# Expert phase of a transformer block on one core: rows routed in normalised form, first layer in two-part weights, 39 tiles in place of 40

## What is computed

```python
x = x + layernorm(attention(layernorm(x)))
x = x + layernorm(ffn(layernorm(x)))

def ffn(f):                                   # f = layernorm(x), 128 wide
    expert = argmax(f @ centroids.T)
    alpha  = sigmoid(max score)
    h = (f - mean(f)) * rsqrt(var(f) + 1e-5) * gamma[e] + beta[e]
    y = f + relu(h @ W1[e].T + b1[e]) @ W2[e].T + b2[e]     # hidden width 512
    return alpha * y + (1 - alpha) * f
```

## Time and profile before

| | us |
|---|---|
| median of 3 timed runs | 1307.07 (1305.11 to 1332.18) |
| the profiled execution: its time | 1304.03 |
| its span, first to last instruction | 1302.2 |
| attention phase, to the last matrix product of a block | to about 1083 |
| handover (last block's routing, filling rows, table) | about 1083 to 1104 |
| expert phase, first load to last store | 1103.9 to 1293.9 |

### The profile page before, as it was taken

One profiled execution on the slowest core, in us unless ns is written; L12 is line 12 of the kernel. 1 busy time (PEld: TensorE's weight loads), 2 busy tenths in 40 slices (PEclk: granted clock), 3 DMA queues, 4 the chain that ended last, 5 costly groups with the idle time before them and its releaser, 6 DMA issues.

```text
span 1302.2 us, 40447 instructions
## 1 busy us (share of the span) xinstructions
PE 1239.2 (95%) x12156; PEld 1101.3 (85%) x12156; DVE 1157.4 (89%) x4556; ACT 1058.5 (81%) x3176; POOL 923.2 (71%) x1442
## 2 busy tenths in 40 slices
PE   6999999999999999999999999999999995999992
PEld 4898999989998998889899899989999884788782
DVE  4999999999999999999999999999999883799993
ACT  4998888888888888888888888888888882666661
POOL 3567777777777777777777777777777563488886
PEclk8999999999999999999999999999999996999996
DMA  5000000000000000000000000000000003121120
GB/s 221 6 10 14 13 12 12 12 12 12 12 12 12 12 12 12 12 12 12 12 12 12 12 12 12 12 12 12 12 8 9 10 10 84 50 64 59 58 61 4
DMA packets 38504, 31.88 MB, mean 24 GB/s; under 512 B 4882, under 2 KB 35734, under 8 KB 38080
## 3 DMA queue, kind: packets, MB, share of 16 engines
q1 hardware_dynamic: 31696, 21.47, 5.5%
q0 software_dynamic: 4656, 8.81, 2.0%
q10 hardware_dynamic: 2112, 1.11, 0.3%
HBM read 20.35 MB, written 12.07 MB: 25 GB/s over the span
## 4 chain that ended last, share of the span: by engine, by line
PE 81%; DVE 9%; issue 4%; POOL 3%; ACT 1%; DMA 1%; SPq 0%; POOLq 0%; DVEq 0%; ACTq 0%
PE psZU L654 17%; PE psS L591 14%; PE psZU L669 14%; PE psP L623 10%; PE psZU L657 7%; PE psT L605 5%; PE psT L606 5%; PE psT L607 4%; DVE ff L373 2%; DVE wup_s L390 2%; POOL out L452 1%; DVE on L399 1%; DVE gg L408 1%; PE psM L697 1%; PE psM L706 1%
## 5 line engine op out<-in xcount | busy, mean ns | idle before, releaser
L1123 POOL TENSOR_TENSOR prob<-prob,rinv 128x256 f32<-128x256 f32 (+1 forms) x512 | 412.6, 827 | 253.3 <-DVE rinv L886 252.6
L745 ACT ACTIVATE prob<-nscore,nmax 128x128 f32<-128x128 f32 (+1 forms) x1024 | 452.4, 450 | 3.3 <-DVE nmax L868 3.0
L868 DVE CUSTOM_DVE_ANT_0 nscore<-psS,mask 128x128 f32<-128x128 f32 (+1 forms) x1024 | 322.7, 353 | 2.6 <-PE psS L591 1.6
L877 DVE TENSOR_TENSOR p_lo<-psP,p_hi 128x768 fp32r<-128x768 f32 x256 | 243.6, 951 | 3.0 <-ACT p_hi L715 3.0
L715 ACT ACTIVATE t_hi<-psT 128x512 fp32r<-128x512 f32 x256 | 152.9, 597 | 114.0 <-PE psT L607 113.4
L856 DVE TENSOR_TENSOR t_lo<-psT,t_hi 128x512 fp32r<-128x512 f32 x256 | 176.4, 689 | 63.6 <-ACT t_hi L715 63.3
L715 ACT ACTIVATE p_hi<-psP 128x768 fp32r<-128x768 f32 x256 | 206.8, 808 | 3.3 <-PE psP L623 3.3
L745 ACT ACTIVATION_READ_ACCUMULATOR prob<-nscore,nmax 128x1 f32 x1024 | 199.6, 195 | 0.0
L891 DVE TENSOR_TENSOR z_lo<-psZU,z_hi 128x512 fp32r<-128x512 f32 x256 | 174.2, 681 | 10.3 <-ACT z_hi L715 2.7
L591 PE MATMUL psS<-t_hi,t_lo 64*128 64x128 f32 (+1 forms) x1024 | 164.7, 317 | 0.6 <-DVE nmax L868 0.6
L605 PE MATMUL psT<-xt_hi,qk_lo 128*128 128x256 f32 x512 | 155.4, 304 | 3.7 <-DVE t_lo L856 2.3
(11 more groups left out here) (173 smaller groups left out, 3263.6 us busy)
## 6 DMA issues: line engine op xcount, KB each, us to landing
fin<-routed_rows SPq DMA_DIRECT2D x40, 136.0 KB, 2.2
wx<-ffn_w SPq DMA_DIRECT2D x2, 2058.0 KB, 12.7
xin<-x SPq DMA_DIRECT2D x32, 128.0 KB, 2.2
xres<-x SPq DMA_DIRECT2D x32, 128.0 KB, 2.1
out<-res,fin POOLq DMA_INDIRECT x80, 2.2
routed_rows<-padr ACTq DMA_DIRECT2D x4, 272.0 KB, 5.2
routed_rows<-padr SPq DMA_DIRECT2D x4, 272.0 KB, 4.4
wup_s<-wup SPq DMA_DIRECT2D x1, 1024.0 KB, 4.9
```

The source lines that it names most:

```text
L745: last = nc.scalar.activation(prob[:, pb, h, a:z], nscore[:, (s - lag) % 2, h, a:z], ACT.Exp, bias=nmax[:, pb, h, q:q + 1], scale=-1.0, ac ...
L868: last = v.tensor_tensor_reduce(nscore[:, n1, h, a:z], psS[:, h, a:z], mask[:, a:z], -1.0, -MASKED, ALU.add, ALU.min, nmax[:, p1, h, q:q + 1])
L877: v.tensor_tensor(by_half(p_lo, s % 2), psPh, by_half(p_hi, s % 2).bitcast(F32), ALU.subtract).then_inc(S["p_split"], 1)
L1123: last = g.tensor_tensor(pr, pr, rinv[:, p2, :, q:q + 1].broadcast_to([P, 2, z - a]), ALU.mult)
```

## The change

A row is now 260 numbers: the twice normalised row (columns 0 to 127), x (128 to 255), `gain` = alpha times the second 1/sigma, `eps` = 1e-5 times the square of the second 1/sigma, the token number. Since a layer norm does not see a common factor if its epsilon is scaled with the square of it, `gg` is formed straight from the normalised row.

- Attention phase: GpSimd writes the normalised row and the scaled epsilon (r = 4), and the gain (r = 7, before the row writes); ACT and DVE work out alpha for each block (r = 6). DVE no longer keeps the score in the row.
- Emptying slots 1 to 8: ACT and DVE split gamma times the first-layer weights of one expert a slot into a high and a low fp32r part (`w1`); the eight in-place multiplications by ACT are gone.
- Expert phase: DVE's `ff`, `nn`, alpha steps and ACT's exponential are gone. PE turns `fin` itself. The turned tile is split into `nt_hi` (ACT) and `nt_lo` (DVE), and the first layer is 3 fp32r products in place of one fp32 product. ACT copies 1024 + 512 + 5 columns of weights and biases a tile in place of 1029. `on`, `res` and the stores come one slot later. GpSimd adds the row's own epsilon.
- 39 tiles, not 40. Most of the new buffers lie in buffers of the attention phase.

```diff
-    TILES += -TILES % 8
...
+C_X = 128
+C_GAIN = 256
+C_EPS = 257
+C_ID = 258
+ROW = 260
...
+                    b = (s - 1) % 2
                     for j in range(FB):
-                        last = mm(psH[:, j, :], wst[:, (s - 1) % 4, j * P:(j + 1) * P], nt[:, (s - 1) % 2, :],
-                                  start=True, stop=True)
+                        for n, (m, nt) in enumerate(((1, nt_hi), (0, nt_lo), (0, nt_hi))):
+                            last = mm(psH[:, j, :], w1st[:, b, m, j * P:(j + 1) * P], nt[:, b, :],
+                                      start=(n == 0), stop=(n == 2))
...
+                    act.wait_ge(S["argmax_steps"], 3 * (b0 + db) - 5)
+                    nc.scalar.activation(ea[:], best[:], ACT.Exp, scale=-1.0).then_inc(S["exp_done"], 1)
...
+                    dve.wait_ge(S["exp_done"], b0 + db - 1)
+                    v.tensor_scalar(ea1[:], ea[:], 1.0, None, ALU.add).then_inc(S["alpha_steps"], 1)
+                    dve.wait_ge(S["alpha_steps"], 2 * (b0 + db) - 3)
+                    v.reciprocal(alpha[:], ea1[:]).then_inc(S["alpha_steps"], 1)
...
+                    g.tensor_tensor(pay[:, db, :, 0:P], fn[:], rstd2[:].unsqueeze(2).broadcast_to([P, 2, P]),
+                                    ALU.mult).then_inc(S["nn_stored"], 1)
+                    g.tensor_tensor(sq2[:], rstd2[:], rstd2[:], ALU.mult).then_inc(S["gain_steps"], 1)
+                    pool.wait_ge(S["gain_steps"], 2 * n - 1)
+                    g.tensor_tensor(pay[:, db, :, C_EPS], sq2[:], eps_t[:], ALU.mult).then_inc(S["gain_steps"], 1)
...
+                    pool.wait_ge(S["alpha_steps"], 2 * n)
+                    g.tensor_tensor(pay[:, db, :, C_GAIN], rstd2[:], alpha[:], ALU.mult).then_inc(S["gain_ready"], 1)
...
+                    nc.scalar.activation(w1[:, s - 1, 0, :], wx[:, s - 1, 0:FB * P], ACT.Copy,
+                                         scale=gam[:, s - 1:s]).then_inc(S["w1_hi_done"], 1)
...
+                    v.scalar_tensor_tensor(w1[:, s - 1, 1, :], wx[:, s - 1, 0:FB * P], gam[:, s - 1:s],
+                                           w1[:, s - 1, 0, :].bitcast(F32), ALU.mult,
+                                           ALU.subtract).then_inc(S["w1_split"], 1)
```

290 lines of the change are left out of this document (143 added, 147 removed).

## The result

The changed kernel takes 1321.09 us, median of 4 runs (1320.13 to 1323.71), where the kernel before takes 1309.13 (median of 4): 1.0102 times as long, 95% interval 1.0078 to 1.0126. Forecast were 1304.5 us, range 1296 to 1315. The time came out above the range: the profiled execution went from 1304.03 to 1320.32 us, its span from 1302.2 to 1318.5, +16.3 us where my sum said -0.9.

The account below looks back on a forecast made before the run. PE was taken to bound attention, GpSimd at about 4.2 us a tile the expert phase. Terms -4.2 + 2.0 + 0.7 + 0.6 gave -0.9 us on a 1302.2 us span; forecast median 1304.5 us, range 1296 to 1315.

Parts of the forecast that it names:

- What bounds each phase: Attention: PE, busy 987.5 of 990 us. Expert phase: GpSimd at about 4.2 us a tile, with DVE level.
- Tiles, -4.2: Expert phase: one tile fewer saves one pass of GpSimd's five instructions, -4.2 us.
- Pace, 0: Expert phase, time per tile: DVE and PE relieved, GpSimd's five instructions unchanged at about 4.2 us, so 0.
- Handover, +0.7: Between attention and expert phase: extra small steps and doubled row bytes, less ACT's removed multiplications: +0.7 us (-0.4 to +2.5).
- Attention, 0: Attention phase: additions on GpSimd, ACT and DVE vanish in their idle time beside PE: 0 (0 to +11 us).
- rival 3: Attention: the additions reach PE, with ACT's exponential and alpha in r = 6; up to 11 us, 1309 to 1316; chance 0.08.
- Start of the kernel, +0.6: Kernel start: GpSimd fills a wider `padr` and has one more step before PE's first transposes: +0.6 us.
- Start of the expert phase, +2.0: Up to the first store: it comes one pipeline slot later, some earlier steps get shorter: +2.0 us (+0.5 to +3.5).
- 1 (ACT the bound): Expert-phase loop: ACT's slot grows to 4.45 us and sets the pace; 9 us more, 1313; chance 0.12.
- 2 (GpSimd faster beside an idler DVE): Expert phase: GpSimd speeds up without `ff` and `nn` beside it, pace 3.95 us; 9.5 us less, 1295; chance 0.09.
- a new stall between the phases: Example under "anything else", beside a pace over 4.9 us; no size given; chance 0.04 for all of it.

Follow-up runs that it names:

- a3: Changed kernel with the sum with the residual in the expert phase done by DVE behind its normalisation instead of by GpSimd: 1305.16 us.
- b1: Kernel before the change with 39 tiles instead of 40 and nothing else: 1306.45 us.
- c4: Changed kernel with the gain made by DVE behind alpha instead of by GpSimd in front of the first row write: 1313.59 us.
- a1: Changed kernel with ACT's last copies of the experts' first-layer weights ahead of its four filling-row DMAs: 1311.15 us.
- d1: Changed kernel with ACT's last weight copies ahead of its filling-row DMAs and the sum with the residual on DVE: 1301.89 us.
- d2: Changed kernel with ACT's last weight copies ahead of its filling-row DMAs, and both the residual sum and the gain on DVE: 1296.88 us.
- c1: The changed kernel run once more with nothing edited: 1319.90 us.
- c2: Changed kernel with ACT's last weight copies ahead of its filling-row DMAs, residual sum on DVE, and GpSimd's padding-row fill moved behind its constants: 1305.79 us.
- c3: Changed kernel with 15 more waits on ACT before attention, on a semaphore already there, so only ACT's instructions lie further on: 1320.55 us.

## Why the prediction was wrong

*What bounds each phase: right.* DVE lost 35 us of 150 and nothing came of it by itself; a3 takes 0.74 us of a tile from GpSimd, and the tile gets 0.26 us shorter. On the order of GpSimd's instructions: the root and the sum that uses it are one tile apart in both kernels (tiles s-3 and s-4 before, s-4 and s-5 now), so no lag was added between them, against what I wrote beside the change; the whole chain from `gg` on comes one slot later.

*Tiles, -4.2: right* (b1). *Pace, 0: mis-sized.* The tile became 0.06 us longer, and the whole stretch gave -1.0 instead of -4.2. Of these 3.2 us some 1.7 are the long first stores, 27 of them; 0.9 is one slot of 5.14 us, and two slots of 4.48 and 4.54 make 0.5 (a slot of 4.9 to 5.0 us is in both kernels). I had the store of 1.10 us in front of me in the earlier trace rows and read it as one with DVE idle. DVE was not idle there: it had waited for the root and was starting the normalisation. My own list of what the profile would show has DVE waiting for the root in every tile, and I did not put the two together.

*Handover, +0.7: this is a step that failed*, in its last sentence: "The split of the weights in the emptying slots (0.6 us each on ACT and DVE a slot) lies in ACT's and DVE's pauses of those slots, since PE is what they wait for." For the first six pieces no run shows a large cost, though none tests them alone: to the filling rows c4, in the quick rhythm and without the gain on GpSimd, takes 0.7 us more than the kernel before. The last two stand behind ACT's filling-row DMAs, whose 5.21 us of issue are in the earlier trace rows; I priced those DMAs by their bytes and never as time on ACT's queue. Moving the copies ahead gave back 2.95 of 4.8 us (a1), the gain on DVE another 0.9 (d1 to d2), and d2 is 0.6 above the kernel before. On the doubled bytes I had two readings, 15 us by the rate, which "hold up the last row writes by 1 to 2 us", or 8 by the number of rows, and took the middle at no cost. The rate was right: the filling rows land 15.6 us after their first issue. That cost nothing in the changed kernel only because ACT's queue had delayed the last block by more, which is luck. Where the queue is put right it costs 1.3 us (a1) and 1.1 (d2). With the copies ahead (a1) the stretch is 1.85 us above the kernel before, inside my -0.4 to +2.5.

*Attention, 0: failed too, 6.6 us with its end.* I added up the busy time of the additions and compared it with idle time; neither mattered. What came were two things that busy times do not show. First, GpSimd's row write now follows an instruction whose result it waits for, and starts 0.97 us behind it where it had started 0.17 after the previous instruction: once at the start and again to the filling rows, 1 and 1.9 us, since in between PE sets the pace (c4). Second, the slow rhythm: 27 x 0.12 to 0.19, 3.3 to 5.2 us; what brings it is open. My rival 3 had a price for attention (1309 to 1316) but a mechanism, alpha on ACT and DVE, which the runs refute: the kernels in the quick rhythm have the exponential and alpha in them and take the 32.70 us of the kernel before (a1, a3), and c4 gives DVE one instruction more and the block stays at 32.71.

*Start of the kernel, +0.6: right for what it named, and short by what it left out.* From the fill of `padr` to PE's transposes GpSimd's list takes 2.35 us (1.77 before). In the whole the first row write came 3.0 us later. Between ACT's first copy of turned probabilities after 60 us (at 61.42 before, 63.34 now) and the row write lie 50.5 us in the changed kernel and in a1, and 49.4 in the kernel before and in c4: 1.1 us for the wait on the gain. About 1.3 us are the fall of the clock, seen in c1 and a1. These are not exact to tenths: b1, with the code of the kernel before up to there, writes its first row 0.9 us earlier than that.

*Start of the expert phase, +2.0: right in mechanism and size.* Rows landed to first store, from where the forecast counts, is 23.2 us (20.85 before, +2.35); the landing of the longer rows takes 2.9 instead of 2.2, of which 0.3 stood under the handover. The first layer of tile 1 ran at the low clock, as I had feared. How much depends on that show windows of four us, the changed kernel first, then a1:

```profile
1118.30:1122.30 4.00, 0.69 (x2) 0.29 (x2) 0.00 (x0) 0.99 (x3) 0.00 (x0) 0.50 0.50 135
...
1126.30:1130.30 4.00, 2.93 (x14) 2.94 (x14) 0.74 (x2) 2.11 (x5) 0.00 (x0) 0.50 0.65 184
1130.30:1134.30 4.00, 4.00 (x27) 3.79 (x27) 1.70 (x4) 3.37 (x8) 0.00 (x0) 0.96 0.00 0
```

```profile
1110.10:1114.10 4.00, 0.69 (x2) 0.29 (x2) 0.00 (x0) 0.39 (x2) 0.00 (x0) 0.50 0.52 139
...
1118.10:1122.10 4.00, 2.91 (x20) 2.78 (x21) 1.69 (x5) 3.33 (x9) 0.00 (x0) 0.96 0.63 184
```

At 0.50, the level of 1.2 GHz, the changed kernel stays through the third window, 8 to 12 us after the first load; a1 has left it by then and stores 1.4 us earlier. The other traces bear it out: with 260-number rows the two kernels that have left the low level in that window (a1 at 0.96, a3 at 1.00) need 24.7 and 24.1 us to the first store, the thirteen traces at 0.50 need 25.3 to 26.9. Which of them leave it early is not explained.

The time is 6.1 us above the range. Neither the handover (4.1 us beyond its term) nor the slow rhythm of attention (3.3 to 5.2) accounts for that alone; a1, without the one and the other, is at 1311.15, inside it.

*Rivals.* 1 (ACT the bound): no, GpSimd has no waits and ACT is busy 115 of 150 us. 2 (GpSimd faster beside an idler DVE): no, none of its instructions got shorter by more than 0.01 us and its first store is 0.07 us longer. Of what the Trainium skill (page "SBUF — State Buffer", section "Who interferes with whom") says of the shared ports the runs agree with the rule for two inputs, in a3. The rival that won, a queue that is filled with DMAs and address loads, with work behind it on which another engine depends, was in the list only as "a new stall between the phases", with a chance of 0.04 for all that was left.

*What stays open:* what decides between the rhythms. The same program gave the slow one in both of its traces; of the other kernels with the gain on GpSimd and its order kept, two were slow (c2, c3) and seven quick, without a pattern in the clock at 38 to 42 us (slow at 0.57 to 0.76, quick at 0.50 to 1.00), in the gap, which all have, or in the time of the first row write (slow at 112.12 to 116.69, quick at 111.90 to 115.04). And why GpSimd's store is 0.06 to 0.07 us longer when DVE's normalisation starts just before it: the coincidence has no exception in the traces, the cause was not tested.

## What to carry to other kernels

Price a DMA twice: by its bytes, and by the time for which it and what prepares it hold the queue of the engine that issues it (1.3 us each on ACT here: 0.43 to 0.53 for the DMA instruction, most of the rest for loading its address); then list what stands behind it on that engine and who waits for that. When one delay is gone, look for the one that it hid: here the landing of the filling rows. A step put in front of a DMA costs more than its duration if the DMA waits for its result (0.97 us of wait for a 0.2 us product); give it to another engine that has room.

Relieving engines beside the one that never waits gains nothing by itself, but it can make room. In the kernel before DVE was busy 143.5 of 150 us, which leaves under 0.2 us a tile; the sum that a3 gives it takes 0.42. It was the relief of DVE that let the sum go there (that it would not have paid in the kernel before was not run). With that move and three small ones the 12 us lost became 12 us won.

## What the runs showed that I had not expected

- A pipelined loop of 4 us slots ran in one of two rhythms, 32.7 and 32.8 us a block (32.89 in one trace), in kernels whose loops are the same; with waits that wait for nothing, ahead of the loop, it came out in the other one in two of three cases. A comparison of two kernels within 0.4% can be one of rhythms.
- GpSimd's first store of 128 rows takes 1.10 us when DVE's normalisation starts 0.15 or 0.16 us before it and 1.04 or less otherwise, without exception in 664 stores.
- A GpSimd root of 128x2 takes 0.72 us, and up to 1.00 when a DVE sum with both inputs in SBUF starts with it or up to 0.15 us before it; a sum that starts after the root does not touch it.
- DMAs at the head of a queue, with the loads of their addresses, delayed a block's statistics by 5.5 us though nothing on the DMA engines was waited for.
